# Another order for the first part of a fused attention and feed-forward kernel: values and x1 of two chunks ahead of K, weight and bias preparation spread out behind them

## The reference

```python
xn = ln(x, ln1_g, ln1_b);  q, k, v = split(xn @ w_in.T + b_in)          # 16 heads of 16
allowed = (idx % 8 == 0)[:, None] | (idx[:, None] == idx[None, :])
o = softmax(where(allowed, q k^T / 4, -inf)) v;  a = x + o @ w_out.T + b_out
a = a + gelu(ln(a, ln2_g, ln2_b) @ w1.T + b1) @ w2.T + b2               # 256 -> 1024 -> 256
y = layernorm(x + a)
# second layer: top-1 of 8 experts; an expert is the base map plus a rank-4 addition
z = layernorm(y + (relu(y @ wi.T + wi_b + lora_of_top1(y)) @ wo.T + wo_b))
```

## Time and profile before

| what | value |
|---|---|
| median of 3 runs | 1451.54 us |
| the profiled execution, its own time | 1452.35 us |
| span of its records | 1450.6 us |
| PE busy | 1404.0 us, 97% |
| DVE busy | 846.5 us, 58% |
| ACT busy | 721.7 us, 50% |
| POOL busy | 649.0 us, 45% |
| mean granted clock of PE | 0.993 |

### The profile page before, as it was taken

One profiled execution on the slowest core, in us unless ns is written; L12 is line 12 of the kernel. 1 busy time (PEld: TensorE's weight loads), 2 busy tenths in 40 slices (PEclk: granted clock), 3 DMA queues, 4 the chain that ended last, 5 costly groups with the idle time before them and its releaser, 6 DMA issues.

```text
span 1450.6 us, 26449 instructions
## 1 busy us (share of the span) xinstructions
PE 1404.0 (97%) x10167; PEld 1063.0 (73%) x10167; DVE 846.5 (58%) x1792; ACT 721.7 (50%) x1071; POOL 649.0 (45%) x533
## 2 busy tenths in 40 slices
PE   6889999999999999999999999999999999999997
PEld 4778655678888766668888866666888875557996
DVE  7747676636656666555647575763566556762332
ACT  3444555554444555554444555555344455555442
POOL 4554321338754414145865431333776441132755
PEclk9899999999999999999999999999999999999999
DMA  7464123215561222212682213220556212310100
GB/s 251 158 177 103 50 51 66 55 41 190 186 163 44 58 59 50 55 44 81 205 211 69 76 31 79 55 55 16 166 188 166 87 38 50 79 26 23 52 15 30
DMA packets 91393, 130.50 MB, mean 90 GB/s; under 512 B 8314, under 2 KB 68180, under 8 KB 88148
## 3 DMA queue, kind: packets, MB, share of 16 engines
q1 hardware_dynamic: 91268, 128.82, 32.2%
HBM read 68.08 MB, written 60.57 MB: 89 GB/s over the span
## 4 chain that ended last, share of the span: by engine, by line
PE 78%; DVE 11%; POOL 5%; issue 2%; ACT 1%; DMA 1%; SPq 0%; POOLq 0%; DVEq 0%; ACTq 0%
PE ps L1550 19%; PE ps L1551 16%; PE ps L1552 16%; PE ps L1739 9%; PE ps L1728 6%; PE ps L1713 4%; DVE mx L1428 3%; PE ps L1787 2%; DVE stats L1302 2%; PE ps L1775 2%; PE ps L1809 2%; POOL rows L1034 2%; PE ps L1745 1%; PE ps L1671 1%; DVE xn L1390 1%
## 5 line engine op out<-in xcount | busy, mean ns | idle before, releaser
L1428 DVE TENSOR_REDUCE mx<-ps 128x2 f32<-128x1024 f32 x256 | 311.1, 1223 | 189.9 <-PE ps L1713 188.3
L1157 ACT ACTIVATE prob<-ps 128x1024 f32<-128x1024 f32 x256 | 261.8, 1023 | 139.1 <-PE ps L1728 138.8
L1049 POOL TENSOR_TENSOR hid1l<-gel,hid1h 128x512 fp32r<-128x512 f32 x85 | 111.3, 1310 | 207.1 <-ACT hid1h L1199 206.9
L1049 POOL TENSOR_TENSOR hid2l<-gel,hid2h 128x512 fp32r<-128x512 f32 x85 | 111.4, 1311 | 201.6 <-ACT hid2h L1199 201.6
L1049 POOL TENSOR_TENSOR hid0l<-gel,hid0h 128x512 fp32r<-128x512 f32 x86 | 112.5, 1308 | 194.2 <-ACT hid0h L1199 194.2
L1191 ACT ACTIVATE gel<-ps,cols 128x512 f32<-128x512 f32 x128 | 88.1, 688 | 181.0 <-PE ps L1552 169.9
L1739 PE MATMUL ps<-prob,vals 128*32 128x256 f32 x2048 | 163.6, 391 | 0.0
L1193 ACT ACTIVATE gel<-ps 128x512 f32<-128x512 f32 x128 | 76.5, 598 | 170.6 <-PE ps L1809 170.6
L1728 PE MATMUL ps<-qslot,kslot 50*128 50x256 f32 x1024 | 128.9, 330 | 1.8 <-ACT prob L1157 1.8
L1728 PEld LDWEIGHTS ps<-qslot,kslot 50*128 50x128 f32 x1024 | 76.2, 184 | 66.5 <-issue 46.9
L1713 PE MATMUL ps<-kslot,qslot 48*128 48x512 f32 x512 | 102.3, 410 | 3.5 <-DVE mx L1428 3.0
(11 more groups left out here) (244 smaller groups left out, 3956.5 us busy)
## 6 DMA issues: line engine op xcount, KB each, us to landing
k_d<-kst SPq DMA_DIRECT2D x192, 128.0 KB
kslot<-k_d SPq DMA_DIRECT2D x64, 384.0 KB
xin<-in_L_attn_x SPq DMA_DIRECT2D x32, 256.0 KB, 4.0
rows<-xs_d SPq DMA_DIRECT2D x16, 512.0 KB, 6.0
y_d<-rows SPq DMA_DIRECT2D x15, 512.0 KB, 3.1
rows<-y_d SPq DMA_DIRECT2D x15, 512.0 KB, 4.3
out<-rows SPq DMA_DIRECT2D x15, 512.0 KB, 3.9
xs_d<-xin SPq DMA_DIRECT2D x28, 256.0 KB, 2.7
```

The costliest lines, as they stand in the source:

```text
L1049: nc.gpsimd.tensor_tensor(hid[i % RING][1][:], gel[i % 2][:], hid[i % RING][0][:], ALU.subtract).then_inc(lo_done, 1)
L1157: nc.scalar.activation(prob[(n - 1) % 2][:].rearrange("p e i q -> p (e i q)"), ps[:, 0:2, :].rearrange("p a n -> p (a n)"), ACT.Exp).then_ ...
L1428: nc.vector.tensor_reduce(best[:, :, j % NQ], ps[:, at:at + 2, :], AX.X, ALU.max).then_inc(maxr_done, 1)
```

## The change

The step `setup` is gone. Its content becomes steps of their own: `vt` (vectors), `bs` 2, 1, 0 (row sums of b_in for values, K and Q, two sums each), `cv` (the columns for the constant row), `wl` (the low part of w_out, on DVE alone). The nine pieces before the items become a list written out by hand; the b1 sums are cut into 2, 3 and 3, of which the last two stand inside the first two items; the transposes `pt` of the fourth chunk move behind the first `up`. The weight groups are renumbered (w_out is group 0) and get other PSUM banks. The DMA of w_out is issued ahead of that of w_in.

```diff
-            now = {0: (5, 6, 7), 1: (8, 9)}
-            for j in range(9):
-                piece(*todo.pop(0))
-                for g in now.get(j, ()):
-                    put(("wt", g))
-                for s in {5: [("l2a", k), ("bi", 0)], 6: [("l2b", k), ("bi", 1), ("tn", k, 0)], 7: [("tn", k, 1)],
-                          8: [("pa", b, CHUNKS[4])]}.get(j, []):
-                    put(s)
+            one, two, three, four = CHUNKS[:4]
+            for s in [("pa", b, one), ("pb", b, one), ("wt", 0), ("pt", b, one), ("vt",),
+                      ("pa", b, two), ("wt", 1), ("wt", 2), ("bs", 2), ("pb", b, two), ("cv",), ("wt", 3), ("wt", 4),
+                      ("wt", 5), ("pt", b, two), ("pv", b, one, 0), ("pv", b, one, 1), ("xc", b, one), ("bs", 1), ("bs", 0),
+                      ("vx", b, one), ("pa", b, three), ("xc", b, two), ("pk", b, one), ("stk", b, one), ("stx", b, one),
+                      ("pb", b, three), ("pv", b, two, 0), ("pv", b, two, 1), ("vx", b, two), ("l2a", k),
+                      ("wt", 6), ("pt", b, three), ("pk", b, two), ("stk", b, two), ("stx", b, two), ("ldx", b, CHUNKS[4]),
+                      ("l2b", k), ("wt", 7), ("wt", 8), ("pk", b, three), ("wt", 9), ("tn", k, 0), ("tn", k, 1),
+                      ("pv", b, three, 0), ("bi", 0), ("stk", b, three), ("xc", b, three), ("pa", b, four), ("pv", b, three, 1),
+                      ("pb", b, four), ("vx", b, three), ("ldx", b, CHUNKS[5]), ("pa", b, CHUNKS[4])]:
+                put(s)
+            todo = todo[9:]
+            extra = {0: [("bi", 1)], 1: [("bi", 2), ("wl",)]}
...
-            if now:
+            if now and (b or j):
                 piece(*now.pop(0))
             for g in weights.get(j, ()):
                 put(("wt", g))
+            if not b and j == 0:
+                put(("pt", b, CHUNKS[3]))
...
     if k < FIRST:
-        return (2, 0, 1, 3, 4, 5)[k]
+        return (7, 0, 1, 4, 5, 6)[k]
     if k < MEND:
-        return OUT + k % 4 if k < BIAS_AT else DOWN + k % 2
+        return (5, 6, IN, 5, 6, OUT, 6, OUT)[k - FIRST]
     return OUT
...
+                        if i < len(BIASES):
+                            act.wait_ge(d_setup, D_AT[("bi", i)])
                         nc.scalar.activation(gel[i % 2][:], ps[:, UP, :], ACT.Gelu, bias=cols[:, B1C + f:B1C + f + 1]).then_inc(act_done, 1)
```

More of the change, by code:

```diff
@@ L410, in build_steps @@
     put(("lw", 2))
[L411 to L415, removed]
     for b in range(B):
@@ L486 @@
     _banks = []
-    if _w == "wt":
+    if _w == "vt":
+        _banks = [6]
+    elif _w == "wt":
         _banks = [bank_of(_s[1])]
@@ L560 @@
 KCP = [_n // B for _n in KCP]
-COLS, BIN_DONE, CVB = 2, 9, 16
-A_SETUP = 25
 def setup_groups():
-    g = [("qk", k) for k in range(KT)] + [("wout", 0)] + [("vo", k) for k in range(KT)] + [("crow", 0)]
+    g = [("wout", 0)] + [("qk", k) for k in range(KT)] + [("vo", k) for k in range(KT)] + [("crow", 0)]
     g += [("upM", i) for i in range(4)] + [("dnM", i) for i in range(4)]
@@ L578, in casts @@
 def casts(k):
-    return k + 1 + (2 <= k < 5)
-def lows(k):
[L585 to L591, removed]
+    return k + 1 + (k < FIRST - 1)
+D_AT = {}
+_n = 0
+for _s in STEPS:
+    if _s[0] == "wt" and _s[1]:
+        what = SG[_s[1]][0]
+        _n += 0 if what == "bst" else 6 if what == "ga" else 1
+    elif _s[0] == "bi":
+        _n += BIASES[_s[1]][1] - BIASES[_s[1]][0] + 1
+    elif _s[0] in ("vt", "bs", "cv", "wl"):
+        _n += {"vt": 2, "bs": 3, "cv": KT, "wl": 1}[_s[0]] + (_s == ("bs", 0))
+    else:
+        continue
+    D_AT[("wt", 0) if _s[0] == "wl" else _s] = _n
+def lows(k):
+    return D_AT[("wt", k)]
 def attention_ffn_kernel(nc, x, w_in, b_in, w_out, b_out, w1, b1, w2, b2, ln1_g, ln1_b, ln2_g, ln2_b,
@@ L788, in load_weights @@
                 if part == 0:
+                    sp.dma_start(nwout[:], w_out.rearrange("(m p) d -> p m d", p=P)).then_inc(wload[1], 16)
                     sp.dma_start(nwin[:], w_in.rearrange("(m p) d -> p m d", p=P)).then_inc(wload[0], 16)
-                    sp.dma_start(nwout[:], w_out.rearrange("(m p) d -> p m d", p=P)).then_inc(wload[1], 16)
                     for t, v, n in ((G1, ln1_g, KT), (G2, ln2_g, KT), (BIN, b_in, 6), (B1C, b1, FT)):
@@ L1086, in group @@
                                              ps[0:UROWS, at, :].rearrange("u (m p) -> u m p", p=P), ACT.Copy).then_inc(a_setup, 1)
[L1087 to L1090, removed]
             def step(what, *a):
                 b = a[0] if a else None
-                if what == "setup":
-                    setup()
-                elif what == "wt":
+                if what == "wt":
                     group(b)
@@ L1213, in link, with vectors @@
                     dve.wait_ge(d_setup, chain[0])
-            def setup():
+            def vectors():
                 dve.wait_ge(p_ident, 2)
@@ L1218, in setup, with bias_in, spread @@
                 dve.wait_ge(vturn, 1)
-                link(nc.vector.tensor_copy(cols[:, 0:18], ps[:, 7, 0:18]))
-                assert chain[0] == COLS
+                link(nc.vector.tensor_copy(cols[:, 0:18], ps[:, 6, 0:18]))
+            def bias_in(part):
                 dve.wait_ge(wload[0], 16)
                 dve.wait_ge(wload[2], 32)
-                for m in range(6):
+                lo, hi = KT * part, KT * part + KT
+                for m in range(lo, hi):
                     link(nc.vector.tensor_tensor_reduce(out=junk[:], in0=nwin[:, m, :], in1=lnb[:, 0, :], scale=1.0, scalar=0.0,
                                                         op0=ALU.mult, op1=ALU.add, accum_out=cols[:, BINS + m:BINS + m + 1]))
[L1227 to L1231, removed]
+                link(nc.vector.tensor_tensor(cols[:, BIN + lo:BIN + hi], cols[:, BIN + lo:BIN + hi], cols[:, BINS + lo:BINS + hi],
+                                             ALU.add))
+                if part == 0:
+                    link(nc.vector.tensor_scalar(cols[:, QB:QB + KT], cols[:, BIN:BIN + KT], float(HD) ** -0.5, None, ALU.mult))
+            def spread():
                 dve.wait_ge(p_const, 2 + E)
@@ L1234, in setup, with biases @@
                     link(nc.vector.tensor_scalar(cvb[:, k, :], vals[:, 0:P], cols[:, BIN + 4 + k:BIN + 5 + k], None, ALU.mult))
[L1235 to L1243, removed]
+            def biases(part):
+                dve.wait_ge(wload[4], 16)
+                dve.wait_ge(wload[10], 16)
+                lo, hi = BIASES[part]
+                for m in range(lo, hi):
                     link(nc.vector.tensor_tensor_reduce(out=junk[:], in0=nw1[:, m, :], in1=lnb[:, 1, :], scale=1.0, scalar=0.0,
                                                         op0=ALU.mult, op1=ALU.add, accum_out=cols[:, B1S + m:B1S + m + 1]))
-                if half == 1:
-                    link(nc.vector.tensor_tensor(cols[:, B1C:B1C + FT], cols[:, B1C:B1C + FT], cols[:, B1S:B1S + FT], ALU.add))
+                link(nc.vector.tensor_tensor(cols[:, B1C + lo:B1C + hi], cols[:, B1C + lo:B1C + hi], cols[:, B1S + lo:B1S + hi],
+                                             ALU.add))
             def lora():
@@ L1362, in step @@
                 b = a[0] if a else None
-                if what == "setup":
-                    setup()
-                elif what == "wt":
+                if what == "vt":
+                    vectors()
+                elif what == "bs":
+                    bias_in(b)
+                elif what == "cv":
+                    spread()
+                elif what == "wl":
+                    group(0)
+                elif what == "wt" and b:
                     group(b)
@@ L1603, in group @@
                     last.then_inc(pe_setup, 1)
[L1605 to L1610, removed]
             def bank_free(*s):
                 for what, *a in EARLIER.get(s, []):
-                    if what == "wt":
+                    if what == "vt":
+                        pe.wait_ge(d_setup, D_AT[("vt",)])
+                    elif what == "wt":
                         pe.wait_ge(a_setup, casts(a[0]))
@@ L1654, in step @@
                 b = a[0] if a else None
-                if what == "setup":
-                    setup()
+                bank_free(what, *a)
+                if what == "vt":
+                    pe.wait_ge(wload[3], 64)
+                    nc.tensor.transpose(ps[:, 6, 0:18], vecs[:], ident[0:18, 0:18]).then_inc(vturn, 1)
                     return
-                bank_free(what, *a)
                 if what == "wt":
-                    if FIRST <= b < BIAS_AT and bank_of(b) < FIRST:
-                        pe.wait_ge(d_setup, lows(bank_of(b)))
+                    if b == 0:
+                        pe.wait_ge(p_ident, 2)
                     group(b)
```

37 lines of the change are left out of this document (21 added, 16 removed).

## The result

The changed kernel is slower: 1452.7 us, the median of 22 runs (1449.9 to 1455.4), against 1449.35 us of the kernel before in 22 runs beside it. The ratio is 1.0019, with a 95% interval of 1.0012 to 1.0026. I had forecast 1449.7, a gain of 1.8 us; 1452.7 lies inside the range, but on the other side of no change. (The three runs that the forecast started from, 1451.5, were 2 us above what the kernel before takes over many.)

The account below looks back on a forecast made before the run. PE, 97% busy, was taken as the bound, its hole filled only as far as DVE runs ahead. Lead 6.8 us less 3.8, half rate and collisions left 0.4 to 2.4; taking 1.8, 1451.54 became 1449.7 us, range 1445.3 to 1453.5.

Parts of the forecast that it names:

- The 9.1 us hole: PE's wait for block 0's normalized rows, delivered at 42.5 us; priced 11.8 us with its slow stretch, expected to go.
- the 2.64 us wait for the low part of `tn` part 0: PE stands 2.7 us, until 37.7, as part 1 shares the bank; a half-rate stretch follows, 1.4 lost.
- the 2.58 us wait for the fourth chunk: PE idles 2.75 us before the fourth chunk's K at 47.6; a half-rate stretch costing 1.3 to 1.7 follows.
- the 3.0 that I had left at K4: Lead remaining at the fourth chunk's K: start at 47.6 us against 50.57 before, down from 6.8 at `up` 0.
- Giving it back: After `up` 0, work moved behind on DVE cuts the 6.8 us lead to 0.2 to 2.75 by the sixth chunk's K.
- rival B: Gelu 2's gate delays the sixth chunk's low part to 69.2 us, starving PE; slower, 1456 us; chance 0.12.
- DVE's total is unchanged: Argument against the slower rival: DVE's total work stays the same; no separate size given.
- done in the hole: The 3.7 us of DVE work for `bi` 1, `bi` 2 and `wl` was said to run inside the 9.1 us hole before.
- The hole stays and shifts along: PE's 3.0 us hole at block 1's row load persists, moving with the sixth chunk's K low, 1.1 to 1.9 earlier.
- the forecast of both stretches: PE at half rate after the `tn` part 0 and fourth chunk waits; 1.4 and 1.3 to 1.7 us lost.

Follow-up runs that it names:

- e1: The change with only `wl` (low part of w_out) moved from item 1 to between the two parts of `tn`; 1.0024 of the kernel before.
- e2: The change with sums `bi` 1 and 2 moved right behind `pb` of the fifth chunk, ahead of the fourth chunk's K; 0.9989 of the kernel before.
- e4: The change with the old order of the two loads (w_in, then w_out), nothing else; 1.0025 of the kernel before.
- e10: The change without `bi` 1 and 2: six of eight bias sums neither computed nor waited for; 0.9983 of the kernel before.
- e3: The change with both `wl` moved between the `tn` parts and `bi` 1 and 2 behind `pb` of the fifth chunk; 0.9993 of the kernel before.
- e9: The change with `bi` 1 and 2 right behind `bi` 0, ahead of all items; 1.0005 of the kernel before.
- h0: The change's code (new banks, steps, loads) with the old order of pieces, all bias sums ahead of `up` 0; 1.0006 of the kernel before, 1450.7 us.
- h1: h0 with the last six bias sums moved inside items 0 and 1; 1.0036 of the kernel before, 1453.5 us.
- e5: e3 with the first half of the third chunk's values between the two parts of `tn` on PE; 0.9986 of the kernel before, 1446.5 us.
- e7: e5 with the fourth chunk's transposes moved back ahead of `up` 0; 1.0012 of the kernel before, 1450.0 us.

## Why the prediction was wrong

**What held.** The 9.1 us hole went. Statistics of `l2a` started at 30.3 (forecast 27.5, before 33.9) and the order of events up to `up` 0 was the forecast's: the collisions of a `bs` 1 sum (1.42 us), of `pb` of the third chunk (2.79) and of `l2b` (2.6), the 2.64 us wait for the low part of `tn` part 0 (2.7 forecast), the 2.58 us wait for the fourth chunk (2.75), each of the two followed by a stretch at half rate of about 3.4 us. Rows from within these two, and from the stretch behind K6:

```profile
40.90:43.70 2.80, 2.80 (x9) 2.30 (x8) 1.54 (x6) 0.60 (x1) 0.00 (x0) 0.50 0.68 202
50.90:53.50 2.60, 2.60 (x13) 2.60 (x13) 0.86 (x2) 0.00 (x0) 0.39 (x1) 0.50 0.00 0
71.00:74.50 3.50, 3.21 (x16) 2.94 (x15) 3.50 (x5) 1.27 (x3) 2.33 (x2) 0.51 0.37 127
```

**What was off in size.** `up` 0 came at 45.16, not 42.4. All of that was lost before x1 of the first chunk, which ended at 24.7 in place of 21.7: the second chunk's rows came late (DVE waited until 11.33, I had 9.7), and PE was at half rate around the first values, a stretch that the sum does not have. The collisions behind it were counted about right (`pb` of the third chunk 2.79, in the sum 0.74 + 2.2). The 2.8 us ate the 3.0 that I had left at K4: 0.0 was measured. Kernels with the same list up to `tn` part 0 have `up` 0 at 42.65 to 43.98 where the first values ran at full rate (e1, e2, e4, e10) and at 45.12 to 45.90 where they did not (the change, e3, e9), so this term varies from execution to execution by as much as it was missed by.

**The step that failed** is "Giving it back", in its sentence on the moved sums: "Gelu of item 2 waits for `bi` 2 on ACT ... so its low part starts 1.35 after `bi` 2. With the collision and slow stretch it ends at 66.2". I took `bi` 1 as 1.55 us plus a collision of 1.0, let it delay nothing but DVE's own queue, and named no wait of gelu 1 for it. It ended at 62.26, because the sums stand behind x1 of the fourth chunk, which waits for ACT and POOL; gelu 1 was held 4.73 us, and the fifth chunk's K with it; gelu 2 was held 4.33. So the low part ended at 71.5, of which 3.0 is what K4 was already behind the forecast. The collisions themselves were about as counted (1.6 and 0.9 us, in the sum 1.0 and 1.2). The mechanism is that of rival B, with the gate one item earlier than named; I gave it 0.12 and a price of 4.4 us, and it cost 4.7 between `up` 0 and K6 (e2), or 0.30% of the time, 4.3 us (1.0019 to 0.9989; h0 to h1 says the same 0.30%). My argument against it, that DVE's total is unchanged, is the mistake in one sentence: DVE had 13 us free and was still late. (Its busy time did not even stay the same: 49.1 against 45.8 us.) Also, not all of these 3.7 us were "done in the hole" before: four of the eight sums ran from 42.29 to 44.15, at its end and behind it, and the low part of w_out at 17.85.

**What was missed.** Bank 7, which costs nothing beside the gates (e1, e3). And "The hole stays and shifts along" does not hold: it shrank to 1.2 us, and 5.2 us of loss at K6 became 3.0 at block 1. What makes the load quicker in one kernel than in another (6.9 us from issue to first reader before, 6.0 after, 5.2 in e5, 7.3 in e9) stays open. And the earlier trace rows were read too closely: a 9 stands for 0.9 or more, and the third slice, with the 3.4 us at half rate behind 85.62, has 0.95 and not full rate.

**The clock.** PE runs work at half rate for 3.5, 5.4 and 3.4 us before, 12.3 altogether, and in four stretches of 3.2 to 3.5 after, about 13.5. At half rate that is 0.6 us more, and one of the four stretches lies in the shadow of the load: the loss is not made of it. The holes of 2.6 us that ended at 40.3 and 50.6 each had such a stretch behind them, e5's 1.2 us had none; the forecast of both stretches held. But the length of a hole does not settle it. At the first values 2.42 us (the change) had a slow stretch behind it, 2.73 (e2) and 2.72 (e4) had none; further on 2.07 (h1, at 63.0) and 2.24 (e7, at 88.9) had one. So it is in part luck that both stretches came as forecast, and one more or less is worth about 1.7 us (an estimate, half of 3.4). The Trainium skill ("TensorE: Matmul & The Clock Gate", Part 1) holds that the moment of the switch also depends on how the hardware's own free-running watch lies against the work. The traces agree in so far as the same hole has a slow stretch in one execution and none in another.

## What to carry to other kernels

When work moves off a critical wait into a queue that "has time", look up who waits for its result and what is queued behind that waiter. Free time in the queue is no cover if it lies ahead of the moved work, in a wait. The best place for such work is inside a wait of its own engine that the profile shows (here 2.6 us behind `pb`): there 3.1 us of sums cost nothing that could be measured, inside the first two items 0.3% of the kernel. And a PSUM bank is busy until its last reader, so a deferred reader must be looked up in the list of banks too.

## What the runs showed of the hardware that was not expected

A DVE operation need not be large to lose to POOL. The last addition of `bi` 2, 128 x 3 elements with both inputs in SBUF, took 1.10 us at 68.39 and 0.16 at 62.10; POOL ran a sum of 1.51 us from 67.96. Two of the three sums of `bi` 1 took 1.08 and 1.38 us beside POOL's sums at 58.59 and 60.03. Without such company 0.42 is the rule: in e2, where POOL ran no sum beside them, all six took 0.41 to 0.43. POOL's three:

```profile
58.59 1.29 POOL L1014 TENSOR_TENSOR xin<-xin,brow 128x512 f32<-128x512 f32 x1
60.03 1.28 POOL L1022 TENSOR_TENSOR xin<-xin,x1o 128x512 f32<-128x512 f32 x1
67.96 1.51 POOL L1008 TENSOR_TENSOR x1o<-xin,crow 128x512 f32<-128x512 f32 x1
```
